# Denominators of an attention kernel: odd pair sums added to even ones by an accumulating transfer

## The reference

```python
dot = jnp.einsum('bhdt,bhds->bhts', q, k) / math.sqrt(HEAD_DIM)
dot = mask * dot - (1.0 - mask) * NEG
amap = jax.nn.softmax(dot, axis=-1) * mask
out = jnp.einsum('bhts,bhds->bhdt', amap, v)
```

## Time and profile before

| | us |
|---|---|
| Median of 3 runs | 2536.92 |
| Lowest and highest | 2534.54 and 2538.61 |
| Span of the profiled execution | 2538.4 |
| TensorE busy | 2479.6 (98%) |
| VectorE busy | 1986.1 (78%) |
| GpSimd busy | 1642.1 (65%) |
| ScalarE busy | 1392.0 (55%) |

### The profile page before, as it was taken

The page is one execution under the profiler, slowest core; times in us unless marked ns, Lnnn a source line. Parts: engine busy times, 40 slices in busy tenths (PEclk is TensorE's granted clock), DMA queues, the critical chain, the costliest instruction groups (busy, mean ns, idle before and its releaser), DMA issues.

```text
span 2538.4 us, 40565 instructions
## 1 busy us (share of the span) xinstructions
PE 2479.6 (98%) x13177; PEld 1380.4 (54%) x13177; DVE 1986.1 (78%) x3259; ACT 1392.0 (55%) x2606; POOL 1642.1 (65%) x1259
## 2 busy tenths in 40 slices
PE   7999999999999999999999999999999999999997
PEld 5888888874444444444444444444444444444442
DVE  6767667776788888888888888888888888888885
ACT  3333333315666665666666666666665666666664
POOL 2333333426777777777777777777777777777775
PEclk9999999999999999999999999999999999999999
DMA  6766666653444444444444444444444444444411
GB/s 239 256 244 239 237 237 237 215 183 88 94 97 97 100 102 94 96 91 94 91 97 93 91 91 91 91 91 90 99 91 92 95 99 100 97 98 99 101 47 55
DMA packets 241807, 313.48 MB, mean 123 GB/s; under 512 B 75000, under 2 KB 142648, under 8 KB 241624
## 3 DMA queue, kind: packets, MB, share of 16 engines
q1 hardware_dynamic: 230776, 275.56, 43.2%
q10 hardware_dynamic: 10848, 35.66, 3.9%
HBM read 199.83 MB, written 101.38 MB: 119 GB/s over the span
## 4 chain that ended last, share of the span: by engine, by line
PE 88%; DVE 6%; issue 3%; DMA 1%; POOL 1%; ACT 0%; SPq 0%; DVEq 0%; POOLq 0%; ACTq 0%
PE bank L863 20%; PE bank L848 20%; PE bank L893 19%; PE bank L878 17%; PE bank L904 8%; PE bank L941 4%; DVE part_max L1146 3%; PE bank L933 1%; POOL pair_sum L398 1%; DMA q_st<-qx_scr 0%; DVE y L101 0%; DMA w_nat<-in_L_xattn_Wk_dram 0%; DMA v_scr<-stage 0%; DVE isnan L100 0%; DVE x_raw L1046 0%
## 5 line engine op out<-in xcount | busy, mean ns | idle before, releaser
L398 POOL TENSOR_TENSOR pair_sum<-probs 128x512 f32<-128x512 f32 x1020 | 1279.6, 1287 | 430.8 <-ACT probs L715 430.8
L1146 DVE TENSOR_REDUCE part_max<-bank 128x1 f32<-128x512 f32 x2048 | 1283.0, 682 | 346.4 <-PE bank L878 338.1
L715 ACT ACTIVATE probs<-bank 128x512 f32<-128x512 f32 x2048 | 1071.3, 603 | 655.8 <-PE bank L863 647.4
L863 PE MATMUL bank<-q_st,k_st 100*128 100x512 f32 x2048 | 875.4, 429 | 5.2 <-ACT probs L715 5.2
L878 PE MATMUL bank<-k_st,q_st 98*128 98x512 f32 x2048 | 814.0, 397 | 8.7 <-DVE part_max L1146 6.2
L863 PEld LDWEIGHTS bank<-q_st,k_st 100*128 100x128 f32 x2048 | 386.5, 189 | 513.2 <-issue 270.8
L893 PE MATMUL bank<-probs,v_t 128*32 128x512 f32 x4096 | 546.3, 605 | 0.0
L878 PEld LDWEIGHTS bank<-k_st,q_st 98*128 98x128 f32 x2048 | 388.7, 190 | 112.6 <-DVE part_max L1146 8.7
L389 POOL TENSOR_TENSOR stage_lo<-stage,stage_hi 128x512 fp32r<-128x512 f32 x128 | 185.4, 1473 | 139.5 <-ACT stage_hi L661 138.6
L904 PE MATMUL bank<-pair_sum,ones 128*32 128x512 f32 x2040 | 266.4, 594 | 0.0
L661 ACT ACTIVATE stage_hi<-stage 128x512 fp32r<-128x512 f32 x128 | 80.2, 632 | 205.7 <-DVE stage L1010 143.1
(11 more groups left out here) (112 smaller groups left out, 1969.1 us busy)
## 6 DMA issues: line engine op xcount, KB each, us to landing
k_st<-k_scr SPq DMA_DIRECT2D x96, 512.0 KB
q_st<-q_scr SPq DMA_DIRECT2D x192, 256.0 KB
c_raw<-in_ctx_dram ACTq DMA_DIRECT2D x32, 512.0 KB, 7.1
k_scr<-stage_hi SPq DMA_DIRECT2D x64, 256.0 KB, 2.5
k_scr<-stage_lo SPq DMA_DIRECT2D x64, 256.0 KB, 2.8
v_scr<-stage SPq DMA_DIRECT2D x64, 256.0 KB, 2.9
q_scr<-stage_hi SPq DMA_DIRECT2D x64, 256.0 KB, 2.3
q_scr<-stage_lo SPq DMA_DIRECT2D x64, 256.0 KB, 2.5
```

Source lines behind the costliest of these rows:

```text
L398: nc.gpsimd.tensor_tensor(pair_sum[:, r % 2, h], probs[:, a, h], probs[:, a + 1, h], ALU.add).then_inc(pair_done, 1)
L715: nc.scalar.activation(probs[:, c % PR, h, :], s_bank_of(n, k)[:, :], ACT.Exp).then_inc(exp_done, 1)
L863: nc.tensor.matmul(s_bank_of(n, k)[:, :], k_st[p][0:KS, h, j * P:(j + 1) * P], q_st[p][0:KS, th, h, :], start=True, stop=True).then_inc(sc ...
L1146: nc.vector.tensor_reduce(part_max[:, th, sh, at:at + 1], x_bank_of(n, "tile", k)[:, :], AX, ALU.max).then_inc(max_done, 2)
```

## The change

The sums of an even and the next odd pair are added before TensorE sees them. The odd pair's sums go into a second buffer (two buffers, which are `stage_hi` and `stage_lo` of the first part), the even pair's into one of three (`pair_sum`'s two and `stage`). After an odd pair GpSimd issues a transfer of 1 MB from the odd buffer to the even one that adds to it, and its landing is counted in `four_done`. TensorE has four groups of denominators per quad in place of eight, at slots 35, 51 and at 3 and 19 of the next period, and waits for the transfer. The copies of the denominators come at slots 20 and 52 and the inversions at 27 and 59. SyncE's order changes to fit. The last quad's last group is the even pair alone, and `denominators_last` stays.

```diff
--- before.py
+++ after.py
@@ -185,6 +185,7 @@
         scores_ready = sem("scores_ready")
         exp_done = sem("exp_done")
         pair_done = sem("pair_done")
+        four_done = [sem(f"four_done{i}") for i in range(2)]
         pv_done = sem("pv_done")
         den_done = sem("den_done")
         o_copied = sem("o_copied")
@@ -251,6 +252,10 @@
                 q_st.append(sb(f"q_st{i}", [P, TH, QH, HALF], F32R, at))
             probs = sb("probs", [P, PR, QH, HALF], F32, at)
             pair_sum = sb("pair_sum", [P, 2, QH, HALF], F32, at)
+
+            even_sum = [pair_sum[:, 0], pair_sum[:, 1], stage[:, :, :]]
+            odd_sum = [stage_hi[:, :, :].bitcast(F32), stage_lo[:, :, :].bitcast(F32)]
+            NE, NO, GD = len(even_sum), len(odd_sum), SJ // 2
             o_raw = sb("o_raw", [P, TH, HALF], F32, at)
             den = sb("den", [P, HALF], F32, at)
             inv_b = sb("inv_b", [P, TH, HALF], F32, at)
@@ -389,14 +394,32 @@
                             nc.gpsimd.tensor_tensor(stage_lo[:, e % STG], stage[:, g % STG], stage_hi[:, e % STG].bitcast(F32),
                                                     ALU.subtract).then_inc(qk_lo, 1)
 
+                    def wait_stage_free():
+
+                        for i in range(STG):
+                            pool.wait_ge(v_stored[i], 16 * B * (GV // STG))
+                            pool.wait_ge(qk_stored[i], 32 * B * (2 * GK // STG))
+
                     def add_pair(n, r):
-                        a = 2 * r % PR
-                        if counted(SJ * n + r - 1):
-                            pool.wait_ge(den_done, SJ * n + r - 1)
+                        a, g = 2 * r % PR, GD * n + r // 2
+                        if r % 2 == 0:
+                            to = even_sum[g % NE]
+                            if counted(g - NE + 1):
+                                pool.wait_ge(den_done, g - NE + 1)
+                        else:
+                            to = odd_sum[g % NO]
+                            if counted(16 * (g // NO)):
+                                pool.wait_ge(four_done[g % NO], 16 * (g // NO))
                         for h in range(QH):
                             pool.wait_ge(exp_done, NSLOT * n + 2 * QH * r + QH + h + 1)
-                            nc.gpsimd.tensor_tensor(pair_sum[:, r % 2, h], probs[:, a, h], probs[:, a + 1, h],
+                            nc.gpsimd.tensor_tensor(to[:, h], probs[:, a, h], probs[:, a + 1, h],
                                                     ALU.add).then_inc(pair_done, 1)
+
+                    def add_four(n, r):
+
+                        g = GD * n + r // 2
+                        pool.wait_ge(pair_done, QH * (SJ * n + r + 1))
+                        pool.dma_start(even_sum[g % NE], odd_sum[g % NO], accum_op=ALU.add).then_inc(four_done[g % NO], 16)
 
                     def weigh(m):
 
@@ -414,8 +437,12 @@
 
                     def period(n, p):
                         for r in range(SJ):
+                            if n == 0 and r == 0:
+                                wait_stage_free()
                             if real(n) and (n, r) != (LAST, SJ - 1):
                                 add_pair(n, r)
+                                if r % 2 == 1:
+                                    add_four(n, r)
                             if r == 3 and ordinary(n - 1):
                                 weigh(n - 1)
                                 add_residual(n - 1, 1 - p)
@@ -571,16 +598,15 @@
                         if n > 0 and real(n + 1):
                             stack_k(n + 1, 1 - p)
                             stack_q(n + 1, 1 - p)
+                        if ordinary(n - 2):
+                            turn_y8(n - 2)
                         if ordinary(n - 1):
                             move_den(n - 1, 1)
                             load_res(n - 1, 1 - p)
-                        if ordinary(n - 2):
-                            turn_y8(n - 2)
-                        if ordinary(n - 1):
-                            move_inv(n - 1, 1)
                         if real(n):
                             set_max(n, 1, p)
                         if ordinary(n - 1):
+                            move_inv(n - 1, 1)
                             spread_inv(n - 1, 1)
                         if real(n):
                             load_tm(n)
@@ -590,11 +616,10 @@
                             move_den(n, 0)
                         if ordinary(n - 2):
                             store(n - 2, p)
-                        if real(n):
-                            move_inv(n, 0)
                         if real(n + 1):
                             set_max(n + 1, 0, 1 - p)
                         if real(n):
+                            move_inv(n, 0)
                             spread_inv(n, 0)
                         if n == LAST:
                             load_res(n, p)
@@ -721,7 +746,7 @@
                         nc.scalar.activation(o_raw[:, th], o_bank[:, :], ACT.Copy).then_inc(o_copied, 1)
 
                     def copy_den(m, th):
-                        act.wait_ge(den_done, SJ * m + 4 * (th + 1))
+                        act.wait_ge(den_done, GD * m + 2 * (th + 1))
                         if counted(16 * (2 * m + th)):
                             act.wait_ge(den_moved, 16 * (2 * m + th))
                         nc.scalar.activation(den[:, :], d_bank[:, :], ACT.Copy).then_inc(den_copied, 1)
@@ -761,13 +786,13 @@
                                 exp(n, k)
                             if k == 3 and ordinary(n - 1):
                                 copy_o(n - 1, 1)
-                            if k == 12 and ordinary(n - 1):
+                            if k == 20 and ordinary(n - 1):
                                 copy_den(n - 1, 1)
                             if k == 23 and real(n):
                                 copy_max(n, n, 1, 23)
                             if k == 35 and real(n):
                                 copy_o(n, 0)
-                            if k == 44 and real(n):
+                            if k == 52 and real(n):
                                 copy_den(n, 0)
                             if k == 50 and ordinary(n - 1):
                                 scale_rstd(n - 1)
@@ -894,15 +919,18 @@
                                                     probs[:, c % PR, h, :], start=(j == 0), stop=(j == SJ - 1))
                         last.then_inc(pv_done, 1)
 
-                    def denominators(m, r):
-                        th, i = r // 4, r % 4
-                        if i == 0:
+                    def denominators(m, i):
+                        th, g = i // 2, GD * m + i
+                        if i % 2 == 0:
                             if counted(2 * m + th):
                                 pe.wait_ge(den_copied, 2 * m + th)
-                        pe.wait_ge(pair_done, QH * SJ * m + QH * (r + 1))
+                        if (m, i) == (LAST, GD - 1):
+                            pe.wait_ge(pair_done, QH * (SJ * m + 2 * i + 1))
+                        else:
+                            pe.wait_ge(four_done[g % NO], 16 * (g // NO + 1))
                         for h in range(QH):
-                            last = nc.tensor.matmul(d_bank[D * h:D * (h + 1), :], ones[:, :], pair_sum[:, r % 2, h, :],
-                                                    start=(i == 0), stop=(i == 3))
+                            last = nc.tensor.matmul(d_bank[D * h:D * (h + 1), :], ones[:, :], even_sum[g % NE][:, h, :],
+                                                    start=(i % 2 == 0), stop=(i % 2 == 1 and (m, i) != (LAST, GD - 1)))
                         last.then_inc(den_done, 1)
 
                     def denominators_last():
@@ -962,14 +990,15 @@
                                 times_v(n, p, (k - 7) // 4)
                             if k < 7 and real(n - 1):
                                 times_v(n - 1, 1 - p, 15)
-                        if k % 8 == 3:
-                            if k >= 19 and real(n):
-                                denominators(n, (k - 19) // 8)
-                            if k < 19 and real(n - 1):
-                                if n - 1 == LAST and k == 11:
-                                    denominators_last()
-                                else:
-                                    denominators(n - 1, 6 + k // 8)
+                        if k in (35, 51) and real(n):
+                            denominators(n, (k - 35) // 16)
+                        if k in (3, 19) and ordinary(n - 1):
+                            denominators(n - 1, 2 + k // 16)
+                        if n - 1 == LAST and k == 3:
+                            denominators(LAST, 2)
+                            denominators(LAST, 3)
+                        if n - 1 == LAST and k == 11:
+                            denominators_last()
 
                     def period(n, p):
                         for k in range(NSLOT):
```

(6 more changed lines are left out.)

## The result

The changed kernel takes 2885.88 us (four runs, 2879.83 to 2887.08) where the kernel before takes 2535.97 on the same chip: 1.137 times as long, 95% interval 1.1352 to 1.1388. It is slower by 350 us, outside the range of 2425 to 2600.

The account below looks back on a forecast made before the run. TensorE in program order was taken as the bound: 2538.4 - 109 (groups) + 63 (load wait) + 9 (VectorE) = 2501, predicted as 2500 us because runs lie 1.5 us under the profiled span; range 2425 to 2600, the forecast's own 2465 to 2530.

Parts of the forecast that it names:

- The wait for q in slot 19: TensorE waits for the next quad's q load: 2.1 us in each of 30 periods, 63 us.
- the full gain of the groups: On TensorE: 127 denominator groups fewer at 0.86 us each gain 109 us, 3.5 us a period.
- the 9 us for VectorE in slot 59: Inversion and two rounding steps together ahead of four maxima: 0.3 us, 31 times; bounds 0 and 1 us per period.
- The fourth rival: VectorE's local limits cost 3 us instead of 0.3, so time stays about as before, 2530 to 2540; chance 0.07.
- The row maximum: SyncE's load for the second half (L546), now behind other transfers, lands about when TensorE needs it; costed at nothing.
- The cover: At pair 3's product and residual: 2.6 us before ScalarE's exp would wait, against 1.0 us for GpSimd's issue.
- E: What pair 7's accumulate takes of the transfer engines during the k and q loads: 4.1 us, between 0 and 10.3.
- the slack of 2.0 us: Time between the q load's landing at 1495.6 and TensorE's use in slot 19, one group fewer ahead; 2.8 us today.
- At nothing: Cost of the other three accumulates: 14 to 16 us until TensorE uses them, cover gone if one takes over 12.
- The second rival: k and q loads become the bound at slot 19; slower from E = 5.3 us, 149 us at 10.3; chance 0.24.
- The third: Rival: GpSimd becomes the bound if each issue costs over 2.8 us; +164 us at 5 us; chance 0.09.
- The period over 60.7: Sign that the prediction is wrong: period by the chain above 60.7 us, where 59.6 was expected.

Follow-up runs that it names:

- f5: The kernel before with the odd pairs' groups of denominators left out and nothing else moved: 2476.81 us, ratio 0.9760.
- m1: f5 with inversions, copies of the denominators and SyncE's order moved as in the change, and the spread of the inverses split in four: 2579.51 us.
- j1: The changed kernel without accumulating transfers (odd sums left out), its spread of the inverses split into four transfers of 32 rows: 2596.90 us.
- f1: The changed kernel with the accumulating transfers taken out, odd pair sums missing from the denominators: 2664.18 us, ratio 1.0500.
- e1: The changed kernel with every accumulating transfer cut from 1 MB to 32 KB: 2704.28 us, ratio 1.0658.
- e3: The changed kernel with the transfers behind pairs 3 and 5 cut to 32 KB, those behind 1 and 7 whole: 2854.29 us.
- f2: The kernel before plus four accumulating transfers of 32 KB per quad between buffers nothing reads, no compute engine waiting: 2586.42 us.
- e4: The kernel before plus four accumulating transfers of 1 MB per quad between buffers nothing reads, no compute engine waiting: 2842.96 us.
- h1: The kernel before with one accumulating transfer of 1 MB per quad (pair 5's sums onto pair 4's) and one group fewer: 2704.82 us.

## Why the prediction was wrong

The wait for q in slot 19 was forecast and is there. What failed is the slack that stood against it, the full gain of the groups, the 9 us for VectorE in slot 59, and three terms put at nothing: the transfers in front of the loads, GpSimd's issue and the other accumulates. The runs make a ladder from the kernel before to the changed one (differences of medians). Each price is that of the step on top of those above it; the table by stretches shows that in another order they would be others:

| step | predicted | measured | from |
|---|---|---|---|
| 127 groups fewer | -109 | -59 | before to f5 |
| inversions, copies and SyncE's order moved | +9 | +103 | f5 to m1 |
| groups in other slots, pair sums in other buffers, GpSimd's wait for them at the start | 0 | +17 | m1 to j1 |
| spread on four engines ahead of the loads | 0 | +67 | j1 to f1 |
| four issues on GpSimd, 32 KB each | 0 | +40 | f1 to e1 |
| bytes of pairs 1 and 7 | +63 | +150 | e1 to e3 |
| bytes of pairs 3 and 5 | 0 | +32 | e3 to after |
| sum | -37 | +350 | |

- **The groups removed.** The 0.86 us of a group is right, and each one gone gives it back in its place. But f5 shows that 1.9 us of a period are won (60.8 to 59.0) and not 3.5, because behind slots 11, 43 and 59 TensorE then waits for VectorE's maxima, 1.6 us a period. "What it executes less is gained, up to the point at which another queue is late" was the right condition; the forecast looked for that point in slot 59 alone, at 0.3 us. The fourth rival had this mechanism at 3 us, with a chance of 0.07; the mean busy share of 87% that stood against it says nothing of single slots.
- **VectorE in slot 59.** The place was named, and the price of 0.3 us a period was 3.3 (m1 over f5, all of it in slots 60 to 3). I added durations of one engine's rows and did not look at what GpSimd does at that time. The inversion in front puts L93 0.43 us later, and with slot 59's group gone pair 7's adds begin 0.92 us earlier; the 1.32 us that lay between them became -0.03. I also left out that a stop of TensorE is followed by half a clock.
- **What moves in SyncE's order.** The row maximum, the transfer that I looked at, came in time as forecast (7.9 us of waits in all). What failed is that I did not look at what the loads now have ahead of them. `spread_inv(n, 0)` just ahead of the loads follows from the diff (its inversion four slots later, some 3 us) and from the 3.7 us that its issue had to them. It makes the slack of slot 19 negative before any accumulate is issued: f1 waits there 26 times. It also delays the product in f1 (0.6 us a period).
- **GpSimd's issue.** A gap of 1.0 us ahead of the product was forecast, and 0.91 is measured. The cover was wrong. I took the exp of slot 48 (2.6 us) for the first user; ScalarE's copy in slot 35 waits for the product, and did so before for 68.7 us. It had no cover at all: 0.88 us a period (f2). The 40 us from f1 to e1 are not this price alone, since the stop behind slot 59 went with it and the one at the load grew.
- **The bytes in the load.** E was forecast at 4.1 us for pair 7's transfer alone, and the load came 4.3 us later (17.8 to 22.1) with pair 7's and pair 1's together, each of which took 5.4 us of the engines. So the agreement is luck; in the unmoved schedule the load came 6.5 us later (13.9 to 20.4, f2 to e4). What E was set against failed: the slack of 2.0 us. In the trace of before the load's first half lands at 1497.6, 0.8 us ahead of its use at 1498.43, and not at 1495.6 as I worked out from the mean rate; over the quads this slack is 0.9 us in the median. The last of the 104 landings sets the wait, and in the changed kernel slot 19's matmul starts 0.04 us behind it. And the wait costs the clock too.
- **The other accumulates.** "At nothing" failed for at least one of the three. Pair 1's meets the late load; pair 5's lies before the 8 KB move of the denominators, which lands after 5.63 us, and VectorE's inversion waits for it (29.8 us in all). No run separates pair 3's from pair 5's.
- **GpSimd's wait for the buffers** was in the diff (`wait_stage_free`) and in no term of the sum. It costs some 13 us once (first period 68.9 in j1, 56.0 in m1).

The second rival had the direction, the place and the condition, but priced one place out of several; at the measured 6.9 us a period of this place it would be 207 us in 30 periods, more than its largest price. The third had an engine that does cost, but GpSimd did not have to become the bound of the period for it. The signs given were useful: half of the records, 30 waits at slot 19, "5 us or more the second". "The period over 60.7" is met with 71.2.

## What to carry to other kernels

When an order by hand is moved, list for each queue what now stands ahead of the transfer with the least slack, and for VectorE which of its SBUF to SBUF steps now meet a GpSimd operation; neither is in a sum of durations. Read slack from the last landing and not from bytes by mean rate, and count the clock behind every new stop of TensorE. Two SBUF to SBUF steps of VectorE and GpSimd that start within 0.1 us of each other can swap their order by an edit elsewhere, and here that decided over 0.69 or 1.80 us. A broadcast whose outer dimension is 4 should be cut into rows when it goes out close to a critical load: here this was worth 67 to 155 us, and nothing where it was not close.

## What the runs showed of the hardware

An accumulating transfer of 1 MB within SBUF takes 5.4 us of all 16 engines (5.2 in h1, where it runs in a quiet stretch) and costs GpSimd 0.88 us and 0.3 idle. A plain copy of it takes 3.3 us, and with it the kernel is 2% faster (2829 against 2886 us). A stop of TensorE of 1.87 us was followed by granted clocks of 0.57 and 0.75 in the next two windows of 5 us. VectorE's L93 and GpSimd's add do not run side by side: the one that starts second ends late, by 1.1 us for L93 (m1) and by 0.5 us for the add (e1). With the accumulates of pairs 1 and 7 the loads' first half landed 4.3 us later, though the rate rose to 235 GB/s in one window: the engines moved more than the 204 GB/s of a window of m1 with the loads and no accumulate, and still the loads came late.
